# Attention maximum from half differences, with projections in the two score banks

## The reference, cut to what matters

```python
x = x + cross_attention(layernorm(x), ctx, ctx, length)     # 2048 queries, 1601 keys, 16 heads of 64
x = x + mixture_of_experts(layernorm(x))                    # 8 experts, best 2
# in the attention, per head:
q, k = rope(q_in @ Wq + bq), rope(k_in @ Wk + bk)
scores = q @ k.T / 8                                        # keys at or behind `length` are left out
attn = softmax(scores); out = attn @ v
```

## Time and profile before

| | |
|---|---|
| median of 3 runs | 1438.8 us (1435.45 to 1442.55) |
| the profiled execution, first to last instruction (span) | 1442.7 us |
| what lies around that span | not shown; the runs' median is 3.9 us under the span, so the span stands for the execution's own time |
| mean granted clock of TensorE | 0.910 of 2.4 GHz |
| busy: PE, DVE, POOL, ACT | 1113.4, 1074.6, 705.8, 650.2 us |
| VectorE in attention (120 to 1036 us) | 827.5 of 916 us |

### The profile page before, as it was taken

One profiled execution on the slowest core, in us unless ns is written; L12 is line 12 of the kernel. 1 busy time (PEld: TensorE's weight loads), 2 busy tenths in 40 slices (PEclk: granted clock), 3 DMA queues, 4 the chain that ended last, 5 costly groups with the idle time before them and its releaser, 6 DMA issues. The chain is left out here.

```text
span 1442.7 us, 31703 instructions
## 1 busy us (share of the span) xinstructions
PE 1113.4 (77%) x10244; PEld 727.7 (50%) x10407; DVE 1074.6 (74%) x1836; ACT 650.2 (45%) x1202; POOL 705.8 (49%) x501
## 2 busy tenths in 40 slices
PE   1257888889878888888898988999678615999862
PEld 1223555556546555555555655666467503666531
DVE  6946998899799799899889979999557622444324
ACT  2322555555555554555555545566455401322210
POOL 4232764674485485476467548555447562000142
PEclk9965999999999999999999999999979757999986
DMA  9523121421312312312132131220187221111223
GB/s 339 180 57 91 42 46 36 92 51 25 92 36 52 81 43 53 73 46 45 35 94 51 27 87 37 52 66 12 36 312 248 65 95 60 55 55 51 73 83 106
DMA packets 98003, 114.74 MB, mean 80 GB/s; under 512 B 44957, under 2 KB 78046, under 8 KB 97630
## 3 DMA queue, kind: packets, MB, share of 16 engines
q1 hardware_dynamic: 87454, 86.98, 22.2%
q10 hardware_dynamic: 7360, 17.66, 3.9%
q0 software_dynamic: 3072, 8.39, 1.8%
HBM read 43.61 MB, written 30.02 MB: 51 GB/s over the span
## 5 line engine op out<-in xcount | busy, mean ns | idle before, releaser
L809 DVE TENSOR_REDUCE part_max<-mx 128x1 f32<-128x427 f32 x768 | 419.8, 593 | 75.3 <-PE mx L592 74.2
L717 ACT ACTIVATE prob<-sc 128x512 f32<-128x512 f32 x640 | 349.1, 595 | 228.5 <-PE sc L580 225.1
L896 POOL TENSOR_TENSOR prob_lo<-prob 128x1024 bf16<-128x1024 f32 x128 | 251.2, 1962 | 275.2 <-ACT prob L717 275.2
L592 PE MATMUL mx<-K,Q 128*128 128x427 bf16 x768 | 243.2, 358 | 84.8 <-DVE part_max L809 54.5
L618 PE MATMUL pv<-VV,prob 128*128 128x129 bf16 x2560 | 276.0, 224 | 1.8 <-POOL prob_lo L896 1.6
L620 PE MATMUL pv<-VV,prob_lo 128*128 128x65 bf16 x2560 | 267.0, 196 | 0.0
L580 PE MATMUL sc<-Q,K 65*128 65x512 bf16 x640 | 251.5, 393 | 9.1 <-issue 3.9
L821 DVE TENSOR_TENSOR prob_lo<-prob 128x1024 bf16<-128x1024 f32 x192 | 253.5, 1320 | 6.7 <-ACT prob L717 6.5
L618 PEld LDWEIGHTS pv<-VV,prob 128*128 128x128 bf16 x2560 | 238.1, 100 | 34.0 <-issue 3.6
L620 PEld LDWEIGHTS pv<-VV,prob_lo 128*128 128x128 bf16 x2560 | 233.0, 100 | 27.3 <-issue 3.1
L579 PE MATMUL sc<-Q,K 128*128 128x512 bf16 x519 | 204.1, 393 | 0.5 <-ACT prob L717 0.5
(11 more groups left out here) (182 smaller groups left out, 1905.9 us busy)
## 6 DMA issues: line engine op xcount, KB each, us to landing
we<-in_w_exp ACTq DMA_DIRECT2D x16, 768.0 KB, 5.5
q32s<-q SPq DMA_DIRECT2D x128, 64.0 KB, 2.0
Q<-next_q_hi SPq DMA_DIRECT2D x32, 256.0 KB, 3.7
attention_out<-o_out SPq DMA_DIRECT2D x64, 128.0 KB, 2.0
o_in<-attention_out SPq DMA_DIRECT2D x16, 512.0 KB, 4.9
VV<-next_v SPq DMA_DIRECT2D x16, 322.5 KB, 3.8
q32s<-q SPq DMA_DIRECT2D x128, 40.0 KB, 1.9
K<-next_k_hi SPq DMA_DIRECT2D x32, 160.0 KB, 3.5
```

Of the source, the lines that this page charges most:

```text
L592: ins = pe.matmul(mx[:, bank, 0:pl.width], Q1[a][:, c * QC + qt * P:c * QC + (qt + 1) * P], K1[a][:, k0:k0 + pl.width], start=True, stop=True)
L717: act.activation(prob[:, s % PRING, j, :], sc[n % 2][:], ACT.Exp, scale=HD ** -0.5).then_inc(exp_done, 1)
L809: dve.tensor_reduce(part_max[:, b_ % 2, qt, h:h + 1], mx[:, pl.part_banks(qt, h)[0]:pl.part_banks(qt, h)[-1] + 1, 0:pl.width], mybir.AxisL ...
L896: pool.tensor_tensor(prob_lo[:, s % PRING, 0:g, :], prob[:, s % PRING, 0:g, :], hi_half(prob[:, s % PRING, 0:g, :])[:, :, 1::2], ALU.subtr ...
```

## The change

**The maximum in two halves.** For keys a (first 640) and b (last 640), max(a, b) = a + relu(b - a). GpSimd makes the difference of the key halves once a pair (`key_rise`, `next_kd`), and one more DMA a head puts it into `KD` on partitions 64 to 127. A part is now a whole query tile: four matmuls of 64 rows and 320 columns, two of the differences (`mx_diff`, rows 64 to 127 of the array) in turn with two of the first half (`mx_first`, rows 0 to 63). Only the upper bf16 half of the keys enters. ScalarE takes relu of 640 differences into `above` (`rise`); VectorE adds `mx_first` to it and reduces to one maximum with one fused operation. The final reduction over three parts becomes a copy.

**Banks.** `mx_first` and `mx_diff` have two banks each, both used by one part, and `pj` is gone: a projection unit takes its turn in the two banks of `sc`. `placed` numbers score tiles and units in one sequence, and one semaphore `sc_read` counts their reading.

**Order.** Parts are in slots 4, 0, 1 and 2, none in slot 3, and stand at the end of a slot: scores, `times_v`, unit, part, and in slot 3 the row.

```diff
-        mx = pb("mx", [P, 3, 512])
-        pj = pb("pj", [P, 512])
+        mx_first = pb("mx_first", [P, 2, 512])
+        mx_diff = pb("mx_diff", [P, 2, 512])
...
-                        need(pe, part_read, p, BLOCKS * pl.block_parts, pl.block_parts * b_ + len(pl.parts) * qt + h + 1)
-                        for bank, k0 in zip(pl.part_banks(qt, h), pl.parts[h]):
-                            ins = pe.matmul(mx[:, bank, 0:pl.width], Q1[a][:, c * QC + qt * P:c * QC + (qt + 1) * P],
-                                            K1[a][:, k0:k0 + pl.width], start=True, stop=True)
+                        need(pe, above_made, p, BLOCKS * QT, n)
+                        need(pe, part_read, p, BLOCKS * QT, n)
+                        cols = slice(c * QC + qt * P, c * QC + (qt + 1) * P)
+                        for h in range(2):
+                            keys = slice(h * pl.kc, (h + 1) * pl.kc)
+                            pe.matmul(mx_diff[:, h, 0:pl.kc], Q1[a][HD:P, cols], KD[a][HD:P, keys], start=True, stop=True)
+                            ins = pe.matmul(mx_first[:, h, 0:pl.kc], Q1[a][0:HD, cols], K1[a][0:HD, keys], start=True, stop=True)
                         ins.then_inc(part_ready, 1)
...
+                    def rise(p, b_, qt):
+
+                        n = QT * b_ + qt
+                        need(act, part_ready, p, BLOCKS * QT, n + 1)
+                        need(act, part_read, p, BLOCKS * QT, n - 1)
+                        act.activation(above[:, n % 2, :, 0:pl.kc], mx_diff[:, :, 0:pl.kc], ACT.Relu).then_inc(above_made, 1)
...
-                        dve.tensor_reduce(part_max[:, b_ % 2, qt, h:h + 1], mx[:, pl.part_banks(qt, h)[0]:pl.part_banks(qt, h)[-1] + 1, 0:pl.width],
-                                          mybir.AxisListType.XY, ALU.max).then_inc(part_read, 1)
+                    def part(p, b_, qt):
+                        n = QT * b_ + qt
+                        need(dve, above_made, p, BLOCKS * QT, n + 1)
+                        dve.sem_inc(above_seen, 1)
+                        dve.tensor_tensor_reduce(above[:, n % 2, :, 0:pl.kc], mx_first[:, :, 0:pl.kc], above[:, n % 2, :, 0:pl.kc],
+                                                 1.0, -3e38, ALU.add, ALU.max, part_max[:, b_ % 2, qt:qt + 1]).then_inc(part_read, 1)
...
+                            need(pe, sc_read, pair, pl.turns, place - 1 - pl.turns, least)
...
+                            place = pl.tile_place(n, last)
+                            need(pe, sc_read, p, pl.turns, place - 1)
...
+                        pool.tensor_tensor(next_kd[:, 0:2 * pl.kc], next_hi[1][:, 2 * pl.kc:4 * pl.kc], next_hi[1][:, 0:2 * pl.kc],
+                                           ALU.subtract).then_inc(kd_made, 1)
...
+                        sp.dma_start(KD[a][HD:P, 0:n // 2], next_kd[r, 0:n // 2]).then_inc(k_loaded[a], 16)
```

More of the change, by code:

```diff
@@ L62, in __init__, with placed, tile_place, unit_place @@
         self.units = QK_UNITS + self.v_units
-        if kt * P <= 3 * 512:
-            self.width = -(-kt * P // 3)
-            self.parts = [[min(j * self.width, kt * P - self.width)] for j in range(3)]
-            self.part_slots = 3
-        else:
-            self.width = -(-L // 4)
-            self.parts = [[2 * h * self.width, (2 * h + 1) * self.width] for h in range(2)]
-            self.part_slots = 1
-        self.block_parts = QT * len(self.parts)
-        order = [m % self.groups for m in range(-2, self.groups - 2)]
-        each = [self.block_parts // self.groups] * self.groups
-        for j in sorted(range(self.groups), key=lambda j: order[j] not in self.pool_groups)[:self.block_parts % self.groups]:
-            each[j] += 1
-        self.parts_at = [list(range(sum(each[:j]), sum(each[:j + 1]))) for j in range(self.groups)]
+        self.pad = self.units % 2
+        self.lead = self.units + self.pad
+        self.turns = BLOCKS * kt + self.lead
+        self.first_part = self.groups - 6
+        self.places = [self.placed(last) for last in (False, True)]
+    def placed(self, last):
+        place, at = {}, self.lead
+        for s in range(BLOCKS * self.groups + LAG):
+            for n, t in self.tiles_of(s):
+                place["tile", n] = at
+                at += 1
+            for u in range(self.units):
+                if s == self.hook_slot(u) and not last:
+                    place["unit", u] = at
+                    at += 1 + self.pad * (u == self.units - 1)
+        return place
+    def tile_place(self, n, last):
+        return self.places[last]["tile", n]
+    def unit_place(self, u):
+        return self.places[False]["unit", u]
+    def v_before(self, place):
+        for v in range(self.v_units):
+            if self.unit_place(QK_UNITS + v) == place - 2:
+                return v
+        return None
     def tiles_of(self, s):
@@ L88, in parts_of @@
         i, m = divmod(s, self.groups)
-        ahead, at = (2, m - self.groups + 2) if m >= self.groups - 2 else (1, m + 2)
-        return [(i + ahead, n // len(self.parts), n % len(self.parts)) for n in self.parts_at[at]]
-    def part_banks(self, qt, h):
-        n = len(self.parts[h])
-        first = (len(self.parts) * qt + h) % self.part_slots * n
-        return range(first, first + n)
+        return [(i + 1 + (self.first_part + qt < 0), qt) for qt in range(QT) if (self.first_part + qt) % self.groups == m]
     def column_block(self, s):
@@ new lines, in scores @@
+                            v = None if last else pl.v_before(place)
+                            if v is not None:
+                                need(pe, v_lo_made, p, pl.v_units, pl.v_units + v + 1)
+                            if s < LAG and n < 2:
+                                need(pe, v_lo_made, p, pl.v_units, pl.v_units)
+                            pe.matmul(sc[place % 2][:], K1[a][:, k], Q1[a][:, q], start=True, stop=False)
+                            pe.matmul(sc[place % 2][:], K2[a][:, k], Q2[a][:, q], start=False, stop=True).then_inc(scores_ready, 1)
@@ L644, in pair @@
                             slot(p, s, last)
-                            for u in range(pl.units):
-                                if not last and s == pl.hook_slot(u):
-                                    project(p + 1, u, 1)
                     pe.sem_inc(pv_done, PRING)
```

221 lines of the change are left out of this document (122 added, 99 removed).

## The result

The changed kernel takes 1482.71 us (median of 4 runs, 1479.78 to 1487.91) beside 1440.67 for the kernel before in the same comparison: ratio 1.028, 95% interval 1.0255 to 1.0308. It is **slower by 2.8%**; 1390 was forecast, and the measured time lies above the whole range. The profiled execution has a span of 1485.9 us against 1442.7.

A forecast was written before the change was run, and what follows sets the result against it. VectorE alone was taken to set stretches 3 to 5 of a pair, TensorE stretches 2, 7 and 8. From 1442.7, -57 for seven pairs, +5 last pair, +2 start gave 1393 span, 1390 us median; range 1345 to 1455.

The forecast's parts named there:

- The chain step of 2.27: Attention, one part's start to the next: part 0.37, matmul tail 0.17, relu 0.70, fused operation 0.93, handovers 0.10 us.
- Blocks without projections: Attention blocks running no projection units: 11.3 us against 10.75 before, 0.6 slower, with the chain setting the pace.
- The first rival: Attention parts: the row halves do not overlap, a part costs 0.64 to 0.88 us, total 1445 to about 1490; chance 0.17.
- from the last part to `max_col` 2.27 + 0.12: End of a block without projections: one chain step, then 0.12 us, before the row of maxima.
- VectorE's busy time less 2.7: Stretches 3 to 5 of a pair: VectorE's busy time falls 2.7 us each, to 12.5, 13.0 and 14.8.
- each value unit holds the second score tile of the next slot ... some 0.7: Stretch 6, two value units: scores wait some 0.7 us until VectorE has read the bank; 13.4 against 14.81.
- The third rival: Shared score banks: late copies of units stall TensorE 0.7 us for each of 77 units, +54, 1444 us; chance 0.06.
- the sums of 11.3 to 12.3: TensorE's own work in stretches 2 to 6 of a pair: 12.3, 11.8, 11.3, 11.8 and 11.6 us.
- the slack rival: Attention: the chain is slack, blocks follow TensorE's sums, 10.0 us without projections, about 0.9 less in 45 blocks, 1350; chance 0.16.

The follow-up runs named there:

- e10: e8 with each part's relu and fused operation in two halves, both halves standing together at the end of TensorE's slot; 1422.4 us, ratio 0.987 to the kernel before.
- e4: Changed kernel with the matmuls on key differences moved to array rows 0 to 63, where the first keys' are; 1491.3 us, ratio 1.064 to the kernel before.
- e1: Changed kernel with the copy into `max_col` made a reduction over one element; 1418.2 us, ratio 1.011 to the kernel before.
- e6: Changed kernel with the relu over 32 of the 320 columns of each half; 1472.7 us, ratio 1.052 to the kernel before.
- e5: e1 with VectorE doing value read-out, fused operation and `max_col` ahead of cosines and turns; 1400.3 us, ratio 1.000 to the kernel before.
- b1: Kernel before with projections sharing the two score banks, old maxima kept, value read-out moved one slot forward; 1422.9 us, ratio 1.017 to the kernel before.
- e2: Changed kernel with VectorE's fused operation and `max_col` ahead of cosines, turns and value read-out; 1467.4 us, ratio 1.048 to the kernel before.
- e7: e5 with the relu over 32 of the 320 columns of each half; 1374.4 us, ratio 0.982 to the kernel before.
- e11: e10 with the row of maxima made in the block's last slot, behind its scores; 1421.6 us, ratio 0.986 to the kernel before.
- e8: e5 with TensorE's projection unit between the two value tiles of its slot; 1398.7 us, ratio 0.999 to the kernel before.

## Why the prediction was wrong

**What held.** The prices of the pieces: the fused operation 0.82 and 0.08 for its read-out (0.93 for both forecast), the relu 0.70, the part 0.38 up to the next scores, halves that start together. The chain step of 2.27 measures 2.34 (a part at 1000.95, the next at 1003.29). Blocks without projections at 11.33 to 11.60 against 11.3 and 11.4: the forecast's most surprising number, that they get slower with a third less on VectorE, was right. Handing the slot's pace to the chain was right as well: TensorE's slot of 2.06 (e10) fits inside it. The first rival's price was near too (e4).

**The step that failed first**: "from the last part to `max_col` 2.27 + 0.12". The 0.12 is the price of L815, 0.17 with a little overlap, and the diff turns L815 from a reduction into a copy: I priced the new form by the old one's row. The copy took up to 1.91 us beside GpSimd, with the clock falling behind it in stretch 5, and cost 22 us of attention (e1; e6 shows the same hold more often). The fused operation's own read-out, for which the prediction also took 0.17, is another instruction and was priced high enough (0.08). The section of the Trainium skill that the prediction cited (SBUF — State Buffer, Who interferes with whom) frees an instruction with at most one SBUF input only outside the two-port modes, and lists copies among those that can enter them. The prediction left that condition out, and it decides here.

**The second**: "VectorE's busy time less 2.7" in stretches 3 to 5. VectorE's busy time fell by 2.4, 1.1 and 1.9 there, and by 0.1 in stretch 2. Where the maxima's reductions stood, whose 768 rows before lie between 573 and 604 ns, operations with two SBUF inputs now meet GpSimd's: the turns of queries took 59.3 us in all instead of 39.0, those of keys 37.9 instead of 28.3. The earlier trace rows had shown a maximum of 2081 ns for L784, and I used it as a bound for the fused operation, where it didn't apply (its 256 rows lie between 806 and 826), and not for the turns, where it did. And those stand ahead of the fused operation in its slot. The reading that VectorE alone sets stretches 4 and 5 was too strong besides: in the pair read, the clock is 0.90 in both, and another pair of the same trace takes 15.79 and 16.78 there at 1.00 instead of 16.49 and 17.65. With the other order another 20.5 us went (e5 against e1). e5 can't say how much of it is shorter turns and how much the order itself.

**The third**: "each value unit holds the second score tile of the next slot ... some 0.7". TensorE waited 19.4 us for the three units of seven pairs, 2.8 a pair, where 1.4 x 7 = 9.8 was priced: the unit of stretch 5 was left out (0.8), and those of stretch 6 come to 2.0 and not 1.4. With the banks alone (b1) the wait was 27.4 and attention 22.5 us longer, a part of it from the read-out that moved into stretch 5. The third rival had 54 us for 77 stalling units; in b1 three a pair were enough for most of 22. For query and key units nothing was forecast; in the orders of e2 and e5 one of them holds the next scores for 1.1 us a pair (7.7 in all).

**The fourth**, a size: TensorE's own time in the stretches with projections. (The prediction's 8 x 0.085 is 0.68; the 0.70 that it used is what the block of values takes in the trace before.) The slot is 2.06 and not 1.94, four times a block, so the sums of 11.3 to 12.3 in stretches 2 to 6 were 0.5 too low by this alone. In e5's windows TensorE is busy 13.18, 12.84, 12.29, 12.91 and 12.47 where the sums had 12.3, 11.8, 11.3, 11.8 and 11.6: 4.9 a pair too low. The other half of that isn't taken apart; a matmul's tail of 0.17 ahead of every wait counts as busy and is in it. The idle rest of these five windows is 9.9, and the forecast had 10.0. For the same reason the slack rival's 10.0 wasn't in reach: e7 and e10 stop at 11.1, e11 at 10.84.

**The sum.** Attention was forecast at 884.8 - 57 + 5 = 832.8 and came out at 920.7 to 923.9, some 88 to 91 off. The copy is 22 of it and VectorE's order with the turns 20.5. e5 is still 46 over the forecast. TensorE's own time in stretches 2 to 6 is some 34 of that (7 x 4.9, read from the windows of one pair), which no run tests by itself, and stretch 1, 18.9 on the mean of six pairs instead of 18.0, some 6. The value units' 10 beyond their price are not a further term: the waits of stretches 2 to 6 as a whole came out as forecast. In stretch 3 the waits have another cause than forecast: in e5's trace VectorE waits 1.22 us for GpSimd's sines and the turn is then held for 2.31, with GpSimd busy 13.48 of 14.85. That GpSimd is the bound there is argued from the windows, not shown. The 11 us from e8 to e10 are no part of the miss either: half of them lie in blocks that had come out as forecast.

## What to carry to other kernels

When a change replaces an operation by another of the same size, price the new form by a row of that form, and ask for each short VectorE instruction on a chain whether a long GpSimd operation can hold it: a copy of four elements can cost as much as GpSimd's whole instruction. When two users are put on one buffer, look first at the order of the engine that empties it; a read-out queued behind a wait for someone else is a stall of the producer. Work taken from an engine is worth its time only in the stretches where that engine ends last, and there its replacements' longest rows count, not their median.

## What the runs showed of the hardware

- A four-element copy from float32 to bf16 in SBUF takes 0.17 us alone and up to 1.91 when it starts behind a GpSimd operation (19 of 64 in the changed kernel, 47 of 64 in e6, each ending with GpSimd's); a reduction over one element does the same in 0.157 (156 to 158 ns over 64, 22 of them inside a GpSimd operation).
- Two matmuls of 64 rows on separate rows start within 0.02 us of each other, on the same rows 0.13 to 0.14 apart. Going to this shape and back costs about 0.1 us each way on the slot (values 0.80 against 0.70; a part 0.38 up to the next scores, where its two pairs of matmuls start 0.13 apart).
- The fused operation's cost is not proportional: 821 ns for 640 elements, 485 for 320, each with 80 ns for the accumulator's read-out; two halves cost VectorE 0.2 us more than the whole.
- Over stretches 2 to 6 of seven pairs TensorE's granted clock was below 1.00 in 15 of 35 in the changed kernel, 7 in e1, 1 in e5 and none in e7 to e11, while its waits for `part_max` and `max_col` together were 100, 89 and 64 us in the first three. One such stretch costs 0.7 us (stretch 4 of e1: 15.7 at 0.89, 15.0 at 1.00) to 1.5 (stretch 6: 16.77 at 0.90, 15.23 at 1.00). In stretch 4 it was 0.89 in the changed kernel after a wait of 1.9 us, and 1.00 in e1 after one of 1.8: what tips it isn't settled here.
- The changed program's stage behind attention took 408 us on one chip and 366 on another. The granted clock in it was 0.83 and 0.87; whether that is cause or company isn't shown. Attention itself agreed within 0.4%.
